# One head of each pair turned by DMA instead of TensorE in a latent-attention block

## The chip, the cores and the metric

The kernel runs on one core of a Trainium2 chip, in one launch. The metric is the device time of that core in microseconds (us). Five engines work side by side, each through its own instructions in order: TensorE (PE; its weight loads are listed apart as PEld), VectorE (DVE), ScalarE (ACT), GpSimd (POOL) and SyncE (SP), which here issues every DMA. They meet only at semaphores.

## The reference

The input is x of 1024 rows by 512. It is normalised by rows (xn), and the output is x + attention(xn) + experts(xn).

```
q_lat = rmsnorm(xn @ q_a_w, q_a_norm_w)            # 192 wide
q     = (q_lat @ q_b_w) -> 32 heads x (128 + 64)   # q_nope, q_pe; rope on q_pe
ckv   = xn @ kv_a_w                                # 64 latent + 64 for k_pe (rope)
kv    = rmsnorm(kv_lat, kv_a_norm_w) @ kv_b_w      # k_nope, v of 32 heads
scores = (q_nope.k_nope + q_pe.k_pe) * 192**-0.5
idx   = sum over 16 heads of iw * relu(iq . ik)    # the indexer
mask  = top 128 of idx in each causal row
attn  = softmax(where(mask, scores, -inf))
out   = (attn @ v) @ o_w
experts: top 2 of 8 gates, rank 16 each, added in
```

## The kernel before, in words

**Numbers.** A product that must keep 32-bit accuracy is made of three 16-bit ones: each operand is split into a high part (rounded to 16 bit) and a low part (what is left), and high x high, high x low and low x high are added up in PSUM. So every operand of TensorE needs a copy to 16 bit (`copy`, L712, on ACT) and a subtraction (`low`, L929, on DVE).

**Stages.** Projections and the indexer come first (to about 300 us), then the head loop (L658 on TensorE), then the last products with the output weights (L685).

**The head loop.** 32 heads make 16 pairs, and the 1024 query rows make two halves of four tiles of 128 rows. A *unit* is one pair in one half: 8 *steps*, one for each head and tile, in order. There are 32 units (NU): 16 of the low half, whose tiles see 128 to 512 keys, then 16 of the high half, whose tiles see 640 to 1024 keys. 256 steps (STEPS) in all. A step g goes through these hands:

- TensorE: scores of 128 rows by all keys seen (`scores`, L604, matmuls at L621), three steps ahead (AHEAD).
- DVE: `row_max` (L1123, instruction at L1131) adds the mask, scales, writes the tile in fp32 to one of four buffers `pr` and keeps the row's extreme `nmax`.
- ACT: `exp_step` (L879, L883): the exponential in place, with the row's sum, two steps ahead.
- TensorE: turns the probabilities block by block (128 x 128, fp32) into a PSUM bank of psT (L666), up to four blocks a bank.
- ACT: `p_hi_chunk` (L886) copies a bank, scaled by 1024, to the high part in `pT`. DVE: `p_low_chunk` (L1135) makes the low part.
- TensorE: `values` (L631, L640), three matmuls for each block of 128 keys, one step later.

In a step of the high half the turn needs two banks, so two copies on ACT and two subtractions on DVE. Between the steps of a unit stand five smaller jobs on the same three psT banks, in the order of the list RING (L255): "R" and "L" (`q_job`, the rope part and the latent part of the queries two units later, L539 to L543), "V" (`vo_pair`, L628, low half only), "O" (`out_T`, L649, the finished unit turned). `unit_out` (L1141) divides a unit's values by the row sums. In the low half DVE also finds the top 128 of the two largest mask rows between the steps (`top_part`, L1061 and L1068, in MARK_STEPS, 64 parts over steps 0 to 118).

POOL works on the queries two units ahead: rope (L1309 to L1313) and the low parts (L1318, L1322), and L1326 in the low half. SP issues the DMAs that this needs: `swap` (L339, L340: neighbouring rows exchanged), `place` (L349: rows to the other 64 partitions, 4 for each unit), and in the low half the loads at L371 and L372 and the store at L376.

The order is written out by hand in each engine's program; no scheduler changes it.

## Time and profile before

| what | value |
|---|---|
| three runs, us | 965.91, 969.08, 969.91 (median 969.08) |
| the profiled execution | 972.53 us, its span 970.8 us |
| PE busy | 880.3 us, 91% of the span |
| DVE busy | 740.9 us, 76% |
| ACT busy | 645.6 us, 67% |
| POOL busy | 367.4 us, 38% |
| mean granted TensorE clock | 0.972 of full |
| share of the 16 DMA engines in use by the SP queue | 25.4% |

The shares are means over stages that have different limits, so the head loop has to be read by its halves. In the profile's 40 slices TensorE is at 9 tenths in nearly every slice from the 21st on, while DVE is at 8 or 9 from the 7th to the 33rd. The last three slices are the output products, on TensorE alone.

### The profile page before, as it was taken

The page shows a single profiled execution, that of the slowest core. Times are in us where ns is not written, and L with a number is a line of the kernel's source. Part 1 is how long each engine was busy: PE and PEld are TensorE (multiplying, and loading weights), DVE is VectorE, ACT ScalarE, POOL GpSimd, SP SyncE. Part 2 cuts the span into 40 slices and gives each one's busy share as a digit, 9 for nine tenths or more (in the row PEclk, how much of TensorE's full clock was granted, in tenths as well). Part 3 has the DMA queues.
Part 4 walks back from the last instruction along what each step waited for, and adds up shares of the span by engine and source line. Part 5 has one row for each costly group of instructions (what it writes and reads, how often), then busy time and mean ns, then how long its engine had stood idle before and what let it go on. Part 6 is the DMA issues. An engine that isn't in the chain of part 4 may idle for free. (4 is left out here: it accounts for less than half of the span.)

```text
span 970.8 us, 21012 instructions
## 1 busy us (share of the span) xinstructions
PE 880.3 (91%) x7912; PEld 549.2 (57%) x7912; DVE 740.9 (76%) x1625; ACT 645.6 (67%) x1448; POOL 367.4 (38%) x291
## 2 busy tenths in 40 slices
PE   5979989968776989898889999999999999999998
PEld 2545544434443555555555777777777767774443
DVE  5366687899998999999998888888788888881100
ACT  3657799865674786777777777777777777880000
POOL 2093388754453544644554322322322323200000
PEclk9989999988886999999999999999999999999999
DMA  7012211112323145345443221111111111330111
GB/s 234 23 44 78 64 46 53 60 38 64 103 87 101 45 126 136 93 114 137 132 106 105 60 52 45 35 34 34 35 42 38 34 45 42 93 130 1 66 44 43
DMA packets 68259, 69.43 MB, mean 72 GB/s; under 512 B 8000, under 2 KB 50368, under 8 KB 68160
## 3 DMA queue, kind: packets, MB, share of 16 engines
q1 hardware_dynamic: 68160, 68.10, 25.4%
q8 instruction: 63, 1.03, 0.5%
q14 instruction: 36, 0.29, 0.1%
HBM read 36.62 MB, written 6.29 MB: 44 GB/s over the span
## 5 line engine op out<-in xcount | busy, mean ns | idle before, releaser
L712 ACT ACTIVATE arena<-psT 128x512 f16<-128x512 f32 (+4 forms) x516 | 242.8, 512 | 81.7 <-PE psT L666 71.4
L883 ACT ACTIVATE arena<-arena,small 128x512 f32<-128x512 f32 (+7 forms) x256 | 198.5, 775 | 65.0 <-DVE small L1131 64.4
L929 DVE SCALAR_TENSOR_TENSOR arena<-psT,arena 128x512 f16<-128x512 f32 (+3 forms) x392 | 206.2, 553 | 41.2 <-ACT arena L712 40.0
L621 PE MATMUL psS<-keyT,arena 128*128 128x512 f16 (+3 forms) x1152 | 231.7, 329 | 3.3 <-issue 3.3
L1131 DVE CUSTOM_DVE_ANT_0 arena<-psS,bias 128x512 f32<-128x512 f32 (+7 forms) x256 | 191.9, 750 | 37.4 <-PE psS L621 36.3
L666 PE MATMUL psT<-ident,arena 128*128 128x128 f32 x1152 | 177.4, 281 | 2.8 <-ACT arena L883 2.4
L621 PEld LDWEIGHTS psS<-keyT,arena 128*128 128x128 f16 x1152 | 102.9, 98 | 82.2 <-issue 25.8
L507 PE MATMUL psS<-ikT,big 128*128 128x512 f16 (+3 forms) x528 | 113.0, 362 | 30.7 <-DVE bias L1014 27.2
L640 PEld LDWEIGHTS psO<-val,arena 128*128 128x128 f16 x2976 | 109.6, 98 | 36.7 <-DVE arena L929 10.5
L666 PEld LDWEIGHTS psT<-ident,arena 128*128 128x128 f32 x1152 | 123.9, 141 | 4.9 <-ACT arena L883 2.3
L640 PE MATMUL psO<-val,arena 128*128 128x64 f16 x2976 | 118.3, 193 | 5.1 <-DVE arena L929 4.7
L1291 POOL TENSOR_TENSOR bias<-arena,bias 128x768 f32<-128x768 f32 (+2 forms) x48 | 91.3, 1917 | 47.1 <-ACT arena L778 46.5
L507 PEld LDWEIGHTS psS<-ikT,big 128*128 128x128 f16 x528 | 51.8, 105 | 85.0 <-DVE bias L1014 34.9
L1068 DVE MATCH_REPLACE8 bias<-m,bias 128x768 f32<-128x768 f32 (+4 forms) x112 | 89.9, 808 | 0.0
L1061 DVE MAX8 m<-bias 128x8 f32<-128x768 f32 (+4 forms) x112 | 87.4, 816 | 0.4
L1311 POOL TENSOR_TENSOR arena<-arena,sq 128x512 f32<-128x512 f32 x32 | 40.8, 1275 | 118.1 <-DMA arena<-arena 118.1
L929 DVE SCALAR_TENSOR_TENSOR big<-psT,big 128x512 f16<-128x512 f32 (+1 forms) x64 | 41.9, 655 | 40.6 <-ACT big L712 40.1
L1318 POOL TENSOR_TENSOR arena<-arena 128x512 f16<-128x512 f32 x32 | 37.1, 1158 | 88.8 <-DVE arena L1098 88.8
L712 ACT ACTIVATE big<-psT 128x512 f16<-128x512 f32 (+1 forms) x64 | 36.2, 565 | 51.3 <-PE psT L649 23.9
L1322 POOL TENSOR_TENSOR arena<-arena 128x512 f16<-128x512 f32 x32 | 37.8, 1181 | 79.9 <-ACT arena L712 78.8
L1309 POOL TENSOR_TENSOR arena<-arena,cq 128x512 f32<-128x512 f32 x32 | 40.9, 1278 | 71.0 <-ACT arena L712 71.0
L1225 POOL TENSOR_TENSOR arena<-arena 128x512 f16<-128x512 f32 x32 | 37.1, 1159 | 54.8 <-ACT arena L712 54.6
(150 smaller groups left out, 1147.9 us busy)
## 6 DMA issues: line engine op xcount, KB each, us to landing
arena<-arena SPq DMA_DIRECT2D x192, 128.0 KB, 2.4
arena<-in_wiq SPq DMA_DIRECT2D x32, 256.0 KB, 2.7
arena<-in_ow SPq DMA_DIRECT2D x16, 512.0 KB, 4.1
arena<-in_qbT SPq DMA_DIRECT2D x16, 256.0 KB, 2.5
wvo_parts<-arena SPq DMA_DIRECT2D x16, 256.0 KB, 2.7
arena<-in_qpe SPq DMA_DIRECT2D x16, 128.0 KB, 2.9
arena<-in_x SPq DMA_DIRECT2D x8, 256.0 KB, 2.9
out<-arena SPq DMA_DIRECT2D x8, 256.0 KB, 2.0
```

What stands on the lines that cost most here:

```text
L507: last = mm(bank[:, c:c + w], iq[:, a, n, t * P:(t + 1) * P], ikT[:, b, c:c + w], start=(a, b) == (0, 0), stop=(a, b) == (1, 0))
L621: last = mm(bank[:, k:k + w], Q[:, u % 2, a, h, q:q + P], keyT[:, b, h, k:k + w], start=(a, b) == (0, 0), stop=(a, b) == (1, 0))
L640: last = mm(dst, pT[:, g % 2, a, j * P:(j + 1) * P], val[:, b, j, :], start=j == 0 and n == 0, stop=j == nb - 1 and n == 2)
L666: last = nc.tensor.transpose(bank[:, (j % 4) * P:(j % 4 + 1) * P], pr[:, g % 4, j * P:(j + 1) * P], ident[:])
L712: return nc.scalar.activation(dst, src, ACT.Copy, scale=scale)
L883: nc.scalar.activation(pr[:, g % 4, 0:kw], pr[:, g % 4, 0:kw], ACT.Exp, bias=nmax[:, g % 4:g % 4 + 1], scale=-1.0, accum_out=rsum[:, unit_ ...
L929: return v.scalar_tensor_tensor(out=dst, in0=src, scalar=scale, in1=hi, op0=ALU.mult, op1=ALU.subtract)
L1061: v.max(m8[:, slot], bias[:, TOFF[t]:TOFF[t + 1]]).then_inc(tk_max, 1)
L1068: v.match_replace(out=row, in_to_replace=m8[:, slot], in_values=row, imm_value=TAKEN).then_inc(tk_rep, 1)
L1131: v.tensor_tensor_reduce(out=pr[:, g % 4, 0:kw], in0=bank[:, 0:kw], in1=bias[:, TOFF[t]:TOFF[t + 1]], scale=-c_s, scalar=3e38, op0=ALU.add ...
L1291: g.tensor_tensor(row, src[:, 0:P * (t + 1)], row, ALU.add).then_inc(sum_done, 1)
L1309: g.tensor_tensor(rt, raw, cq[:, cs], ALU.mult).then_inc(rot, 1)
```

## The change

In every unit the heads alternate: step s of a unit now belongs to head s % 2 and tile s // 2 (`head_of`, `tile_of`, `col_of`), where before the first four steps were one head. Even steps, the first head, go as before. Odd steps, the second head (`turns`, TURNED), are turned by DMA:

- DVE adds log(1024) to the row's extreme (`nmax_s`, one 128x1 instruction that waits for the one before it), so that the exponential comes out scaled.
- ACT, after the exponential and behind a wait for it, copies the rows as they stand to 16 bit (`rows_hi_`, one instruction of full width).
- POOL subtracts to get the low part (`rows_lo_`, one instruction of full width).
- SP issues one DMA transpose of both parts (`turn`), 2 x (blocks seen) blocks of 128 x 128 in 16 bit, into one of four buffers `cols`.
- TensorE forms the value products four steps later (LAG), so an odd step forms two sets and an even step none.

With this PSUM banks are shared out anew: in the high half the ring uses two banks and the third holds the values of every other unit. `pr`'s buffer is freed by POOL for a turned step. `unit_out` moves from step 0 to step 4 of the next unit and first multiplies the reciprocals by a constant (`scaled`). "O" and "V" change places. The buffers of `ow_s`, `wv_s`, `vo_s` and `vo32` become single to make room; the Q tiles are laid out head first. On POOL and SP the query work of a unit is spread over the steps. At the end the first output product goes ahead of the last two sets of values.

The diff, cut to its core:

```diff
+LOG_PR = math.log(PR_S)
+LAG = 4
+TURNED = ((1, 3, 5, 7), (1, 3, 5, 7))
...
+        rows_low = (ikf[:, 0:S], ikf[:, S:2 * S], view(6784, S, F16))
+        rows_high = (bias[:, 0:S].bitcast(F16), view(6784, 2 * S, F16), ikf)
+        cols_low = [view(at, S, F16) for at in (8832, 9344, 16000, 16512)]
+        cols_high = [view(at, 2 * S, F16) for at in (8832, 16000, 14976, 7808)]
...
         def tile_of(g):
-            return ORDERS[half_of(g)][g % 4]
+            return ORDERS[half_of(g)][g % 8 // 2]
+        def turns(g):
+            return g % 8 in TURNED[half_of(g)]
         def chunks(g):
-            return half_of(g) + 1
+            return 0 if turns(g) else half_of(g) + 1
+        def due(x):
+            return [g for g in (x - 1, x - LAG) if 0 <= g < STEPS and turns(g) == (g == x - LAG)]
...
+            def turn(g):
+                d, nb = TURN_AT[g], tile_of(g) + 1
+                sp.wait_ge(row_lo, d + 1)
...
+                elif d >= 4:
+                    sp.wait_ge(av_mm, summed(BY_DMA[d - 4]))
+                sp.dma_start_transpose(cols_of_turn(d)[:, 0:2 * nb * P].rearrange("p (j q) -> p j q", q=P),
+                                       rows_of_turn(d)[:, 0:2 * nb * P]).then_inc(landed[d % 4], 16)
...
+            for g in range(STEPS):
+                u, s = divmod(g, 8)
+                if turns(g):
+                    turn(g)
+                if s == 1 and 2 <= u + 1 < NU:
+                    place(u + 1, latent, qa_lo, q_lat, 1)
+                if s == 2 and 2 <= u + 1 < NU:
+                    place(u + 1, turned, q_rot, q_tur, 0)
+                if s == 3 and u + 2 < NU:
+                    swap(u + 2)
...
             def values(g):
-                pe.wait_ge(p_lo, TCUM[g + 1])
+                if turns(g):
+                    d = TURN_AT[g]
+                    pe.wait_ge(landed[d % 4], landed_by(d))
+                    src = cols_of_turn(d)[:, 0:2 * nb * P].rearrange("p (s k) -> p s k", s=2)
+                else:
+                    pe.wait_ge(p_lo, TCUM[g + 1])
+                    src = pT[:, FLIP_AT[g] % 2]
...
-                if g:
-                    values(g - 1)
-            values(STEPS - 1)
+                for late in due(g):
+                    values(late)
...
+            def rows_hi_(g):
+                kw, d = P * (tile_of(g) + 1), TURN_AT[g]
+                if d >= 3:
+                    act.wait_ge(landed[(d - 3) % 4], landed_by(d - 3))
...
+                act.wait_ge(exp_done, g + 1)
+                copy(rows_of_turn(d)[:, 0:kw], pr[:, g % 4, 0:kw], 1.0).then_inc(row_hi, 1)
...
-                if g >= 4:
+                if g >= 4 and turns(g - 4):
+                    dve.wait_ge(row_lo, TURN_AT[g - 4] + 1)
+                elif g >= 4:
                     dve.wait_ge(t_mm, TCUM[g - 3])
...
+                if turns(g):
+                    dve.wait_ge(max_done, g + 1)
+                    v.tensor_scalar(nmax_s[:, g % 4:g % 4 + 1], nmax[:, g % 4:g % 4 + 1], LOG_PR, None, ALU.add).then_inc(nmax_done, 1)
...
+            def rows_lo_(x):
+                kw, d = P * (tile_of(x) + 1), TURN_AT[x]
+                pool.wait_ge(row_hi, d + 1)
+                g.tensor_tensor(rows_of_turn(d)[:, kw:2 * kw], pr[:, x % 4, 0:kw], rows_of_turn(d)[:, 0:kw],
+                                ALU.subtract).then_inc(row_lo, 1)
```

TensorE in the high half before: the values of one step (L640), the turn of the next (L666), a query job (L539 to L543), scores (L621), again values and a turn.

```order
L640 MATMUL psO<-val,arena 128x64 x18
L666 MATMUL psT<-ident,arena 128x128 x5
L539 MATMUL psT<-qlT,w1hi 128x512
L540 MATMUL psT<-qlT,w1hi 128x512
L541 MATMUL psT<-qlT,w1lo 128x512
L542 MATMUL psT<-qlT,w2s 128x512
L543 MATMUL psT<-qlT,w2s 128x512
L621 MATMUL psS<-keyT,arena 128x512 x6
L640 MATMUL psO<-val,arena 128x64 x24
L666 MATMUL psT<-ident,arena 128x128 x7
```

TensorE at a like place of the changed kernel (L613 to L617 is the query job, L694 scores, L721 values, L748 the turn, L730 the finished unit turned).

```order
L613 MATMUL psT<-qlT,w1hi 128x512
L614 MATMUL psT<-qlT,w1hi 128x512
L615 MATMUL psT<-qlT,w1lo 128x512
L616 MATMUL psT<-qlT,w2s 128x512
L617 MATMUL psT<-qlT,w2s 128x512
L694 MATMUL psS<-keyT,arena 128x512 x6
L721 MATMUL psT<-val,arena 128x64 x45
L748 MATMUL psT<-ident,arena 128x128 x6
L694 MATMUL psS<-keyT,arena 128x512 x6
L730 MATMUL psT<-ident,arena 128x128 x4
```

Two sets of values (21 and 24 matmuls) stand together behind the scores of an odd step; there is a turn in every other step only.

ScalarE in the high half before: exponentials (L883), each between the copies of a turned step (L712, 512 columns and the rest).

```order
L883 ACTIVATE arena,small<-arena,small 128x1024
L712 ACTIVATE arena<-psT 128x512
L712 ACTIVATE arena<-psT 128x256
L883 ACTIVATE arena,small<-arena,small 128x640
L712 ACTIVATE big<-psT 128x512
L712 ACTIVATE arena<-psT 128x512 x2
L883 ACTIVATE arena,small<-arena,small 128x896
```

ScalarE at a like place of the changed kernel (L972 the exponential, L797 `copy`; a copy to arena, ikT or bias from arena is the new copy of rows).

```order
L972 ACTIVATE arena,small<-arena,small 128x896 x2
L797 ACTIVATE arena<-arena 128x896
L797 ACTIVATE arena<-psT 128x512
L797 ACTIVATE arena<-psT 128x384
L972 ACTIVATE arena,small<-arena,small 128x768 x2
L797 ACTIVATE ikT<-arena 128x768
```

Two exponentials of the same width now stand together, with one full-width copy behind the second and the two copies out of PSUM behind that.

## Rows read from the trace of the kernel before

**Rows 1.** Windows (us, busy and count by engine, clock, DMA share, GB/s).
```profile
339.00:450.00 111.00, 98.63 (x976) 59.69 (x974) 105.71 (x275) 82.89 (x240) 58.12 (x49) 1.00 0.44 117
620.00:710.00 90.00, 90.00 (x1113) 66.16 (x1112) 74.39 (x149) 70.10 (x147) 25.79 (x21) 1.00 0.15 37
```

**Rows 2.** Timeline of DVE, low half, line L1144 (start us, us, instruction).
```profile
338.62 0.19 DVE L1144 RECIPROCAL small<-small 128x8 f32<-128x8 f32 x1
...
449.90 0.18 DVE L1144 RECIPROCAL small<-small 128x8 f32<-128x8 f32 x1
```

**Rows 3.** Timeline of DVE, high half, line L1149.
```profile
556.67 0.69 DVE L1149 TENSOR_TENSOR arena<-psO,small 128x512 f32<-128x512 f32 x1
...
841.98 0.69 DVE L1149 TENSOR_TENSOR arena<-psO,small 128x512 f32<-128x512 f32 x1
```

**Rows 4.** Waits from 540 to 870 us (total us, times, longest).
```profile
ACT arena L712 <- PE psT L666: 63.7, 91, 1.2
...
DVE arena L1131 <- PE psS L621: 31.8, 43, 1.3
```

**Rows 5.** Waits from 339 to 450 us.
```profile
POOL arena L1311 <- DMA arena<-arena: 44.8, 8, 6.5
ACT arena L883 <- DVE small L1131: 26.6, 25, 2.2
```

**Rows 6.** Timeline of the high half, TensorE's matmuls.
```profile
762.60 1.07 PE L666 MATMUL psT<-ident,arena 128*128 128x128 f32 x8
...
763.50 1.14 PE L621 MATMUL psS<-keyT,arena 128*128 128x512 f16 x6
...
764.48 0.69 PE L640 MATMUL psO<-val,arena 128*128 128x64 f16 x18
...
765.00 0.74 PE L666 MATMUL psT<-ident,arena 128*128 128x128 f32 x5
...
765.59 0.38 PE L539 MATMUL psT<-qlT,w1hi 128*128 128x512 f16 x1
```

**Rows 7.** Groups by form from 460 to 870 us (busy us, mean ns; idle before).
```profile
L712 ACT ACTIVATE arena<-psT 128x512 f16<-128x512 f32 x192 | 110.9, 595 | 64.7 <-PE psT L666 64.6
L929 DVE SCALAR_TENSOR_TENSOR arena<-psT,arena 128x512 f16<-128x512 f32 x165 | 110.8, 687 | 23.0 <-ACT arena L712 22.0
...
L883 ACT ACTIVATE arena<-arena,small 128x1024 f32<-128x1024 f32 x32 | 36.8, 1151 | 0.2 <-DVE small L1131 0.2
...
L929 DVE SCALAR_TENSOR_TENSOR arena<-psT,arena 128x128 f16<-128x128 f32 x41 | 11.5, 281 | 0.0
L712 ACT ACTIVATE arena<-psT 128x128 f16<-128x128 f32 x41 | 11.1, 271 | 0.0
```

**Rows 8.** Groups by form of POOL over the whole run.
```profile
L1291 POOL TENSOR_TENSOR bias<-arena,bias 128x1024 f32<-128x1024 f32 x16 | 37.7, 2355 | 29.0 <-ACT arena L778 28.4
L1318 POOL TENSOR_TENSOR arena<-arena 128x512 f16<-128x512 f32 x32 | 37.1, 1158 | 88.8 <-DVE arena L1098 88.8
...
L1236 POOL TENSOR_TENSOR arena<-arena,small 128x128 f32<-128x128 f32 x8 | 2.9, 403 | 0.0
```

**Rows 9.** DMA from 12 to 14.5 us (packets, MB, share of 16 engines).
```profile
DMA packets 2543, 0.51 MB, mean 203 GB/s; under 512 B 2362, under 2 KB 2475, under 8 KB 2543
...
q1 hardware_dynamic: 2543, 0.51, 106.6%
```

**Rows 10.** DMA from 339 to 450 us: queue, packets, MB, share.
```profile
q1 hardware_dynamic: 10080, 12.85, 43.8%
```

**Rows 11.** DMA from 600 to 710 us.
```profile
q1 hardware_dynamic: 3680, 3.93, 15.0%
```

**Rows 12.** DMA over the whole run: the queue; issues by KB and us to landing.
```profile
q1 hardware_dynamic: 68160, 68.10, 25.4%
...
arena<-arena SPq DMA_DIRECT2D x192, 128.0 KB, 2.4
```

**Rows 13.** Timeline of SP's issues, high half.
```profile
604.25 0.60 SPq L340 DMA_DIRECT2D arena<-arena  x1
```

More of the change, by code:

```diff
@@ L381, in _ @@
             load_ow(0)
-            load_ow(1)
-            for u in range(NU - 2):
-                swap(u + 2)
-                place(u + 2, latent, qa_lo, q_lat, 1)
-                place(u + 2, turned, q_rot, q_tur, 0)
-                if 1 <= u <= NP:
-                    store_vo(u - 1)
-                if 1 <= u < NP - 1:
+            for g in range(STEPS):
[8 more added lines that the diff above has]
+                    swap(u + 2)
+                if s == 4 and u + 1 < NP:
                     load_ow(u + 1)
-            for u in range(2):
-                sp.wait_ge(vo_st[u], 16 * NP // 2)
+                if s == 7 and u < NP:
+                    store_vo(u)
             sp.wait_ge(qa_mm, NU)
@@ L658, in _ @@
             for g in range(STEPS):
-                pe.wait_ge(exp_done, g + 1)
+                if not turns(g):
+                    pe.wait_ge(exp_done, g + 1)
                 for use in uses_of(g):
@@ L694, in _ @@
             pe.wait_ge(max_done, STEPS)
-            for t in range(2):
-                products(t, t, range(NP))
-                experts(t, t)
+            products(0, 0, range(NP))
+            experts(0, 0)
+            for g in range(STEPS, STEPS + LAG):
+                for late in due(g):
+                    values(late)
+            products(1, 1, range(NP))
+            experts(1, 1)
             pe.wait_ge(p_lo, TCUM[STEPS])
@@ L896, in ot_evac @@
                 copy(big[:, 0, p, c * CH:(c + 1) * CH], bank[:], O_S / (PR_S * K_S)).then_inc(ot_hi, 1)
-            exp_step(0)
-            exp_step(1)
+            for g in range(AHEAD - 1):
+                exp_step(g)
+                if turns(g):
+                    rows_hi_(g)
             for g in range(STEPS):
+                for use in uses_of(g):
+                    what, at, c = use
+                    if what == "T":
+                        p_hi_chunk(psT[BANK[use]], g, c)
+                if g + AHEAD - 1 < STEPS:
+                    exp_step(g + AHEAD - 1)
+                    if turns(g + AHEAD - 1):
+                        rows_hi_(g + AHEAD - 1)
                 for use in uses_of(g):
@@ L904, in _ @@
                     if what == "T":
[L905 to L907 removed]
+                        continue
                     elif what == "O":
@@ L1334, in _ @@
                     rope_low((8, 13).index(n))
-            for u in range(2, NU):
-                rope_turn(u)
-                q_low(u)
-                rope_low(u)
-                if u - 2 < NP:
-                    vo_low(u - 2)
+            for x in range(STEPS):
+                u, s = divmod(x, 8)
+                if x + 1 < STEPS and turns(x + 1):
+                    rows_lo_(x + 1)
+                if s == 0 and 2 <= u + 1 < NU:
+                    rope_low(u + 1)
+                if s == 3 and u + 2 < NU:
+                    rope_cos(u + 2)
+                if s == 5 and u + 2 < NU:
+                    rope_sin(u + 2)
+                if s == 6 and u < NP:
+                    vo_low(u)
+                if s == 7 and u + 2 < NU:
+                    q_low(u + 2)
 def kernel(**inputs):
```

209 lines of the change are left out of this document (135 added, 74 removed).

## The prediction

> **What bounds the kernel now.** I read the windows first, one in each half of the head loop, because the page's shares mix stages. The first of the two rows [rows 1] is the low half: DVE is busy 105.7 of 111 us (95%), TensorE 89%, ACT 75%, POOL 52%. The second is the high half: TensorE is busy all 90 of 90 us, DVE 83%, ACT 78%, POOL 29%. So two different engines set the two halves, at a granted clock of 1.00 of full in both (the 2.4 GHz level).
>
> Next the length of a unit of 8 steps. In the low half the reciprocal that closes a unit comes at 338.62 and, eight units on, at 449.90 [rows 2]: 13.91 us a unit. In the high half the division comes at 556.67 and, 13 units on, at 841.98 [rows 3]: 21.95 us a unit.
>
> Last the waits. In the high half ACT's copies wait 63.7 us for TensorE's turns and DVE's row extremes 31.8 us for its scores [rows 4]: the others wait for TensorE. In the low half ACT's exponentials wait for DVE, and POOL waits 44.8 us for the swap DMA, 5.6 us of each unit's 13.9 [rows 5].
>
> **What leaves TensorE.** Eight turns of blocks run from 762.60 to the start of the scores at 763.50, 0.90 us, and five from 765.00 to 765.59, 0.59 us [rows 6]. That is 0.103 us a block and 0.07 us a step (eight of them show as 1.07 us busy, since each overlaps what follows). In a high unit the four turned steps have 5 + 6 + 7 + 8 = 26 blocks: 26 x 0.103 + 4 x 0.07 = 2.98 us less. The value products are the same matmuls, only later. A high unit falls to 18.97 us if TensorE stays the bound. In a low unit 1 + 2 + 3 + 4 = 10 blocks go, 1.3 us by the same slope.
>
> **DVE.** A turned step loses its subtractions, 0.687 us for 512 columns and 0.281 us for 128 [rows 7]. For 640 to 1024 columns that is about 0.97, 1.10, 1.24 and 1.37, together 4.7 us a high unit; for 128 to 512 columns 0.28 + 0.42 + 0.55 + 0.68 = 1.9 us a low unit. What is added is small: four 128x1 instructions and one 128x8 product. The trace has none of 128x1 with such a wait; the nearest is the reciprocal of 128x8 at 0.19 us [rows 2]. Bounds 0.08 (free but for a start) and 0.35 (with a stall for the one before it); I take 0.2 each, 1.0 us a unit. Low unit: 105.7/8 = 13.2 busy, less 1.9, plus 1.0, is 12.3; with the 5% of idle that it has now, 13.0. High unit: 74.4/90 x 21.95 = 18.1, less 4.7, plus 1.0, is 14.4, off the path.
>
> **ACT.** It has 70.1/90 x 21.95 = 17.1 us of work in a high unit [rows 1]. For a turned step the two copies out of PSUM (0.595 and 0.27 to 0.595) become one out of SBUF of 640 to 1024 columns. The nearest row for one wide instruction out of SBUF is the exponential, 1.151 us for 1024 [rows 7], against 2 x 0.595 = 1.19 for the two. I take no difference, bounds -0.2 and +0.2 us each. The wait for the exponential just ahead is new; behind it are queued the copies of the next turn, for which DVE and TensorE wait. Price 0.1 to 0.4, taken 0.2 x 4 = 0.8 us. 17.9 us is under 18.97, but only just: what hides it is TensorE, and of the gain 1.1 us a unit is all the cover left.
>
> **POOL.** New are four subtractions a unit. By width 2.355 us for 1024, 1.158 for 512 and 0.403 for 128 [rows 8], so about 7.8 us a high unit and 3.3 a low one. With 25.8/90 x 21.95 = 6.3 and 58.1/8 = 7.3 there now [rows 1], 14.1 of 19 and 10.6 of 13. DVE's next row extreme waits for this subtraction where it waited for TensorE, and behind POOL's wait for the swap DMA the next subtraction is queued. That wait is 5.6 us now; spread over the steps it should be hidden by the two steps between the swap and its use, and costs what is left of it if not.
>
> **DMA.** This is the unknown: the trace has no transpose. A turned step moves two parts (high and low) of each of its blocks, 32 KB each: in a high unit 2 x 26 = 52 such blocks, 1.7 MB, in a low one 20, 0.65 MB. If a row of a block (128 elements of 2 bytes, 256 B) is a packet, each of the 16 engines has 8 packets a block. The nearest row is the stretch of small packets at 12 to 14.5 us: 2543 packets, 2362 of them under 512 B, in 2.5 us at a full queue [rows 9], so 16 x 1.066 x 2.5 / 2543 = 16.8 ns of an engine for each, 0.134 us a block. The other end is the mean over all packets of the run, 0.254 x 16 x 970.8 / 68160 = 57.9 ns [rows 12], 0.46 us a block. The lower end takes four rows in one packet of 1 KB at 16.8 ns, 0.034 us a block. I take 0.134, as the row of like packets. The queue then has 52 x 0.134 = 7.0 us plus 15% of 21.95 = 3.3 [rows 11] of 19 us in a high unit, and 20 x 0.134 = 2.7 plus 43.8% of 13.91 = 6.1 [rows 10] of 13 in a low one. It is hidden. A plain DMA of 128 KB lands 2.4 us after issue [rows 12]; the rows are ready about when TensorE starts the step, and values come four steps later, 9.5 us in the high half and 6.5 in the low. SP's own issue is 0.60 us [rows 13]; 10 in a high unit are 6.0 us, 13 in a low one 7.8. The copy, subtraction and turn together have to be slower than three steps before TensorE or ACT (which waits for the landing three turns back) feels it.
>
> Of this the Trainium skill speaks against the change: "VectorE: DVE Perf Modes", section The three transpose paths, gives 1309 ns for a 128x128 block by DMA and 390 ns by TensorE. By that figure taken block after block the turns of a high unit would be an estimated 52 x 1.309 = 68 us. For TensorE the trace disagrees (0.10 us a block in a row of them), so that figure looks like the time of one block alone; for the DMA no run here shows it. If it held, the turns' rival below would be at its far end.
>
> **The rest.** Single buffers for the output weights: load, product, two copies, subtraction and store follow each other once a unit, with about 13 us for some 10; no cost taken, up to 1 us a low unit if the store is late. Two ring banks in the high half: between two turns there is now a whole step without one, over 2 us, against a copy and subtraction of about 1.8; no cost, up to 0.5 a unit. The end, with two sets of values behind a product: within 1 us.
>
> **The sum.** High: 2.98 less 0.5 for coupling that I can't price (ACT at 94% of TensorE) is 2.45 a unit, x 16 = 39 us. Low: 13.91 to 13.0, 0.9 x 15 units with mask work = 13.5 us. Together 52. The profiled execution took 972.5 us, 3.4 above the median of the runs; on the median, 969.1 - 52 = 917 us.
>
> **Rivals.**
>
> *The other engines take the pace, not the DMAs.* In the high half ACT's wait for its own exponential, and for a landing, costs 0.7 a turned step in place of 0.2: 17.1 + 2.8 = 19.9 us, with some 4% idle 20.7, a gain of 1.25 x 16 = 20 us. In the low half DVE's wait for POOL eats the rest. 969 - 20 = 949 us. For it: ACT's narrow margin, and all engines in order with four buffers. Against it: the exponential is two steps ahead.
>
> *The turns themselves set the pace, and the kernel is slower.* Place: the SP queue, its issue or its 16 engines. The change breaks even where a high unit's queue is as long as the unit is now: (21.95 - 3.3) / 52 = 0.36 us a block. Below 0.31 the gain is whole, so the step between is steep. At 0.40, between that and the slow end of 0.46, a high unit is 20.8 + 3.3 = 24.1, 2.2 x 16 = 34 us more, a low one 8.0 + 6.1 = 14.1, some 4 us in all: 1007 us. At 0.46 it is 24.1 + 3.3 = 27.4 and 9.3 + 6.1 = 15.4: 87 and 24 us more, 1080 us. And if the blocks of a turn went one after another, each at the time in which a whole DMA of 32 to 128 KB could land, over 1 us, it would be above 1500 us. For it: a DMA that writes one element of a row to each partition has no like in the trace, its issue may grow with the number of blocks (a plain one's does not), and the trace shows that packets here do cost 58 ns on the mean. Against it: those packets are 1 KB on the mean, and small ones went at 16.8.
>
> The Trainium skill's page "DMA: Bandwidth & Descriptors", section "Why a DMA increments its semaphore by 16 and not by 1", has a table by which earlier chips issue an SBUF to SBUF transpose in small tiles one after another, 262,144 sequencer cycles for 8,192 of them. The size of a tile isn't given, so no time follows from it; it would be this rival by way of SP, and no row shows it.
>
> **Chances.** The forecast has 0.50, with its own range 903 to 935. The engines' rival has 0.14, of which 0.02 ends within 0.5% of before. The turns' rival has 0.36, of which 0.03 ends within 0.5% and 0.02 is the case of block after block. So faster by over 0.5% is 0.62, within 0.5% (what a measurement can tell from no change here) 0.05, slower 0.33. The range starts at 903, under which 0.05 is left, and runs into the turns' rival to 1020, above which are 0.12.
>
> **What would show it.** Right: high units of 19 to 20 us with TensorE still at 95% or more, low units near 13, the transposes landing within 6 us of issue, no wait of ACT or TensorE for a DMA. TensorE or ACT waiting for a transpose, SP busy most of the unit, or landings over 9 us show the slower rival. TensorE at 90% in the high half with short DMAs shows the other. Wrong is also a low unit that stays at 13.9: then DVE's saving went into waits for POOL.

## The result, and the profile after

The changed kernel takes 1062.07 us (median of 4 runs, 1060.82 to 1064.28) against 969.50 for the kernel before, run beside it (4 runs, 965.91 to 973.71): 1.0956 of it, with a 95% interval of 1.0908 to 1.1003. The forecast was 917 us, the range 903 to 1020. It is slower by 93 us and outside the range.

Where the time went shows in the exponentials, since both kernels do them in the order of the steps and two steps ahead. The division that closes a unit (`unit_out`) can't bound the stretches, because the change moved it by half a unit. The first exponential of unit 0 and of unit 16 (the first of the high half) and the last one, before:

```profile
306.94 0.72 ACT L883 ACTIVATE arena<-arena,small 128x512 f32<-128x512 f32 x1 [5.25 <-DVE small L1131]
...
529.41 1.15 ACT L883 ACTIVATE arena<-arena,small 128x1024 f32<-128x1024 f32 x1 [0.20 <-DVE small L1131]
...
872.32 0.94 ACT L883 ACTIVATE arena<-arena,small 128x768 f32<-128x768 f32 x1
```

The same of the changed kernel.

```profile
305.40 0.72 ACT L972 ACTIVATE arena<-arena,small 128x512 f32<-128x512 f32 x1 [5.53 <-DVE small L1242]
...
557.21 1.15 ACT L972 ACTIVATE arena<-arena,small 128x1024 f32<-128x1024 f32 x1 [2.47 <-DVE small L1242]
...
940.68 0.94 ACT L972 ACTIVATE arena<-arena,small 128x768 f32<-128x768 f32 x1 [0.99 <-DVE small L1247]
```

| stretch | before | after | difference |
|---|---|---|---|
| start to the first exponential of unit 0 | 306.9 | 305.4 | -1.5 |
| from there to the first of unit 16 (low half) | 222.5 | 251.8 | +29.3 |
| from there to the last exponential (high half) | 342.9 | 383.5 | +40.6 |
| from there to the end of the span | 98.5 | 118.3 | +19.8 |
| span | 970.8 | 1059.0 | +88.2 |

All further times of a stretch are measured in this way. For the time of one unit the divisions serve, as in [rows 3]: units 0, 11, 16 and 29 of the changed kernel.

```profile
330.84 0.69 DVE L1265 TENSOR_TENSOR arena<-psS,small 128x512 f32<-128x512 f32 x1
...
507.49 0.69 DVE L1265 TENSOR_TENSOR arena<-psO,small 128x512 f32<-128x512 f32 x1
...
604.33 0.69 DVE L1265 TENSOR_TENSOR arena<-psT,small 128x512 f32<-128x512 f32 x1
...
920.22 0.69 DVE L1265 TENSOR_TENSOR arena<-psO,small 128x512 f32<-128x512 f32 x1
```

A unit takes 176.65 / 11 = 16.06 us in the low half (13.91 in [rows 2]) and 315.89 / 13 = 24.3 in the high one (21.95 in [rows 3]). All further unit times are measured between these divisions. The windows of the two halves (columns as in [rows 1]) show that no engine is full.

```profile
331.00:507.00 176.00, 132.82 (x1222) 74.91 (x1219) 140.79 (x387) 121.07 (x329) 114.22 (x110) 0.91 0.63 145
604.00:920.00 316.00, 262.00 (x3208) 171.63 (x3207) 206.74 (x430) 224.49 (x416) 167.79 (x116) 0.98 0.55 103
```

In the high half TensorE is busy 262 of 316 us (83%; 100% in [rows 1]), ACT 71%, DVE 65%, POOL 53%; in the low half DVE 80% (95% before) and TensorE 75%, at a granted clock of 0.91. The queue and the landings of the transposes (median us in the last column), from the DMA view of 604 to 920 us:

```profile
q1 hardware_dynamic: 94272, 32.12, 53.9%
...
arena<-bias SPq DMA_TRANSPOSE x18, 3.9
arena<-arena SPq DMA_TRANSPOSE x18, 4.0
arena<-ikT SPq DMA_TRANSPOSE x17, 4.2
```

So the turns land in about 4 us, values use them four steps later, and the queue is half idle. The waits from 604 to 920 us (total us, times, longest) name no transpose, but DVE and ACT waiting for each other:

```profile
ACT arena L972 <- DVE small L1247: 59.6, 53, 1.4
DVE arena L1038 <- ACT arena L797: 52.7, 39, 1.8
...
PE psT L748 <- DVE big L1038: 33.5, 13, 2.6
```

L972 is the exponential, L1247 the new shift of the row's extreme, L797 `copy`, L1038 `low`. One pair of steps with 1024 columns, from the timeline of all engines (some rows left out):

```profile
731.23 1.22 DVE L1242 CUSTOM_DVE_ANT_0 arena<-psS,bias 128x1024 f32<-128x1024 f32 x1
...
732.50 0.15 DVE L1247 TENSOR_SCALAR small<-small 128x1 f32<-128x1 f32 x1
...
732.68 1.15 ACT L972 ACTIVATE arena<-arena,small 128x1024 f32<-128x1024 f32 x1 [1.25 <-DVE small L1247]
...
734.02 1.06 ACT L797 ACTIVATE arena<-arena 128x1024 f16<-128x1024 f32 x1
734.98 0.58 ACT L797 ACTIVATE big<-psT 128x512 f16<-128x512 f32 x1
735.15 2.13 POOL L1459 TENSOR_TENSOR arena<-arena 128x1024 f16<-128x1024 f32 x1 [3.92 <-ACT arena L797]
...
735.59 0.69 DVE L1038 SCALAR_TENSOR_TENSOR big<-psT,big 128x512 f16<-128x512 f32 x1 [2.14 <-ACT big L797]
736.20 1.36 DVE L1207 CAST arena<-arena 128x512 f16<-128x512 f32 x1
...
736.34 0.66 PE L748 MATMUL psT<-ident,arena 128*128 128x128 f32 x4 [2.57 <-DVE big L1038]
...
737.03 0.60 ACT L797 ACTIVATE arena<-psT 128x512 f16<-128x512 f32 x1 [0.98 <-PE psT L748]
...
738.68 0.81 DVE L1242 CUSTOM_DVE_ANT_0 arena<-psS,bias 128x640 f32<-128x640 f32 x1
```

This is a closed ring: row extreme, shift, exponential, rows copy (734.02, the new one), the finished unit's copy (734.98) and its low part, which free a ring bank, a turn on TensorE (736.34), its copy (737.03), its low part, and only then the row extreme of the next turned step (738.68). It takes 7.45 us for these two steps (the mean of a unit's four pairs is 24.3 / 4 = 6.1), with all engines idle for parts of it. ACT first sits idle for 1.25 us, waiting for the shift, and then does the rows copy while all others wait for what is queued behind it.

### The profile page after: what moved, and what is told of

It is laid out like the page before. It is cut to its first block, busy times and chain, and to the rows that moved or that the text cites. A ratio compares the mean times of both kernels' runs of the same rounds, so it can differ in the third digit from the quotient of the medians.

```text
span 1059.0 us, 20025 instructions
## 1 busy us (share of the span) xinstructions
PE 844.3 (80%) x7336; PEld 489.9 (46%) x7336; DVE 696.3 (66%) x1593; ACT 659.1 (62%) x1384; POOL 528.9 (50%) x429
## 4 chain that ended last, share of the span: by engine, by line
PE 37%; DVE 28%; ACT 14%; issue 13%; POOL 5%; DMA 1%; SPq 0%; POOLq 0%; ACTq 0%; DVEq 0%
PE psS L766 8%; DVE arena L1242 7%; PE psS L694 7%; ACT arena L972 6%; ACT arena L797 5%; DVE arena L1038 4%; DVE m L1170 4%; DVE bias L1177 3%; PE psT L548 3%; PE psT L748 3%; ACT big L797 2%; PE psS L581 2%; DVE arena L1207 2%; PE psO L721 2%; PE psT L568 2%
## 5 line engine op out<-in xcount | busy, mean ns | idle before, releaser
L972 ACT ACTIVATE arena<-arena,small 128x512 f32<-128x512 f32 (+7 forms) x256 | 198.5, 776 | 144.2 <-DVE small L1247 131.2
L694 PE MATMUL psS<-keyT,arena 128*128 128x512 f16 (+3 forms) x1152 | 236.6, 337 | 12.7 <-issue 9.8
L797 ACT ACTIVATE arena<-psT 128x512 f16<-128x512 f32 (+4 forms) x324 | 156.0, 526 | 45.6 <-PE psT L748 35.5
L1038 DVE SCALAR_TENSOR_TENSOR arena<-psT,arena 128x512 f16<-128x512 f32 x200 | 106.4, 557 | 94.9 <-ACT arena L797 94.4
L694 PEld LDWEIGHTS psS<-keyT,arena 128*128 128x128 f16 x1152 | 106.1, 101 | 103.8 <-issue 37.6
L748 PE MATMUL psT<-ident,arena 128*128 128x128 f32 x576 | 98.2, 292 | 44.1 <-DVE big L1038 42.6
L1459 POOL TENSOR_TENSOR ikT<-arena,ikT 128x512 f16<-128x512 f32 (+5 forms) x64 | 72.3, 1130 | 99.6 <-ACT ikT L797 98.8
L1038 DVE SCALAR_TENSOR_TENSOR big<-psT,big 128x512 f16<-128x512 f32 (+1 forms) x64 | 42.1, 657 | 81.6 <-ACT big L797 81.4
L1459 POOL TENSOR_TENSOR arena<-arena 128x384 f16<-128x384 f32 (+7 forms) x42 | 53.5, 1273 | 74.4 <-ACT arena L797 74.1
L721 PE MATMUL psO<-val,arena 128*128 128x64 f16 x1728 | 68.8, 196 | 25.1 <-DVE arena L1038 25.1
L748 PEld LDWEIGHTS psT<-ident,arena 128*128 128x128 f32 x576 | 63.9, 146 | 51.5 <-DVE big L1038 42.0
L721 PEld LDWEIGHTS psO<-val,arena 128*128 128x128 f16 x1728 | 62.1, 100 | 37.9 <-DVE arena L1038 30.7
L797 ACT ACTIVATE big<-psT 128x512 f16<-128x512 f32 (+1 forms) x64 | 35.9, 561 | 69.5 <-PE psT L730 41.7
L797 ACT ACTIVATE arena<-arena 128x512 f16<-128x512 f32 (+3 forms) x106 | 65.0, 645 | 5.1 <-DMA arena<-in_wiq 1.0
L1459 POOL TENSOR_TENSOR bias<-arena,bias 128x1024 f16<-128x1024 f32 (+3 forms) x22 | 39.1, 1776 | 57.7 <-ACT bias L797 57.7
```

What stands on the lines that cost most here:

```text
L694: last = mm(bank[:, k:k + w], Q[:, u % 2, h, a, q:q + P], keyT[:, b, h, k:k + w], start=(a, b) == (0, 0), stop=(a, b) == (1, 0))
L721: last = mm(dst, src[:, a, j * P:(j + 1) * P], val[:, b, j, :], start=j == 0 and n == 0, stop=j == nb - 1 and n == 2)
L748: last = nc.tensor.transpose(bank[:, (j % 4) * P:(j % 4 + 1) * P], pr[:, g % 4, j * P:(j + 1) * P], ident[:])
L797: return nc.scalar.activation(dst, src, ACT.Copy, scale=scale)
L972: nc.scalar.activation(pr[:, g % 4, 0:kw], pr[:, g % 4, 0:kw], ACT.Exp, bias=shift[:, g % 4:g % 4 + 1], scale=-1.0, accum_out=rsum[:, unit ...
L1038: return v.scalar_tensor_tensor(out=dst, in0=src, scalar=scale, in1=hi, op0=ALU.mult, op1=ALU.subtract)
```

## The experiments

Theories: **ring**, the order on ACT and DVE as above; **turns**, the prediction's rival, the DMA or SP's issue; **small edits**, the shift and the product with constants. In the expectations the ring is theory L, its part in the ring banks B, the turns T; O is the new order of heads and buffers, Q queries placed late, P the product, E the late loads. Medians, each against the kernel before in the same batch:

| kernel | us | of before | 95% | low unit | high unit |
|---|---|---|---|---|---|
| e1 max first | 1110.17 | 1.1414 | 1.1373-1.1455 | 15.5 | 27.9 |
| e2 copy later | 1002.88 | 1.0314 | 1.0275-1.0353 | 15.3 | 21.1 |
| e3 both | 1109.12 | 1.1428 | 1.1356-1.1500 | 15.5 | 27.9 |
| e4 second turn | 1104.17 | 1.1342 | 1.1282-1.1402 | 18.6 | 24.2 |
| e5 no turns | 1075.82 | 1.1081 | 1.1036-1.1127 | 14.95 | 27.7 |
| e6 e2, no shift | 998.31 | 1.0292 | 1.0237-1.0347 | 15.5 | 20.9 |
| e7 e2, jobs first | 980.33 | 1.0096 | 1.0058-1.0134 | 15.25 | 19.9 |
| e8 e2, high only | 998.88 | 1.0289 | 1.0235-1.0343 | 14.95 | 21.2 |
| e9 e7, queries first | 962.66 | 0.9900 | 0.9849-0.9950 | 14.5 | 19.7 |
| e10 e5, no product | 1057.74 | 1.0867 | 1.0805-1.0928 | 13.95 | 27.2 |
| e11 e9, tensor_scalar | 962.70 | 0.9908 | 0.9872-0.9945 | 14.4 | 19.7 |
| e12 e11, high only | 959.50 | 0.9858 | 0.9809-0.9907 | 13.65 | 19.7 |
| e13 after, loads early | 1044.90 | 1.0762 | 1.0719-1.0805 | 16.1 | 24.3 |
| e14 e11, loads early | 954.85 | 0.9806 | 0.9769-0.9843 | 14.5 | 19.7 |
| e15 e12, loads early | 945.64 | 0.9737 | 0.9714-0.9761 | 13.6 | 19.8 |

### e1, e2, e3: which order closes the ring

e1, on DVE: the row extreme goes ahead of the low parts of the step's turn.

```
+                if g + AHEAD < STEPS:
+                    row_max(g + AHEAD)
                 for use in uses_of(g):
                     if what == "T":
                         p_low_chunk(psT[BANK[use]], g, c)
-                if g + AHEAD < STEPS:
-                    row_max(g + AHEAD)
```

> On DVE the row extreme of step g+3 now goes ahead of the subtraction(s) of step g; nothing else differs from the changed kernel (1062 us; 24.0 us a high unit, about 15.9 a low one). Theory L (a loop between DVE and ACT sets the pace: subtraction of g, row extreme of g+3, its shift, exponential of g+3, copy of its rows, a small job's copy, copy of the turned g+2, subtraction of g+2): the subtraction leaves the piece ahead of the exponential, up to 1.2 us of each pair of steps in the high half and 0.5 in the low, so high units near 21 to 22 us, low near 14.5 to 15, in all 1000 to 1025 us. Theory B (two ring banks in the high half make TensorE wait): the banks come free later, so high units stay at 24 or grow, low ones stay; 1060 or more. Theory T (the DMA turns set the pace): no change, 1062.

e2, on ACT: the rows copy of a turned step is done one step later, ahead of that step's exponential.

```
+                if g and g + AHEAD - 2 < STEPS and turns(g + AHEAD - 2):
+                    rows_hi_(g + AHEAD - 2)
                 if g + AHEAD - 1 < STEPS:
                     exp_step(g + AHEAD - 1)
-                    if turns(g + AHEAD - 1):
-                        rows_hi_(g + AHEAD - 1)
```

> On ACT the copy of a turned step's rows moves from right behind its own exponential to behind the copy out of PSUM of the next step. Theory L: the copy (0.75 to 1.06 us and the 0.25 of its wait) leaves the piece between the exponential and the next copy out of PSUM, in both halves: high units 21 to 22 us, low near 15, in all 1005 to 1030 us. Theory B: the small jobs' copies come earlier and free their banks about 1 us sooner, so the high half gains and the low half, with three banks, does not: 1030 to 1045. Theory T: the turns start a step later, so the same or up to 10 us slower.

e3 has both edits.

> Both order changes at once. Theory L: the two gains add up until TensorE or ACT is the bound, high units 20 to 21 us, low 13.5 to 14.5: 965 to 995 us. Theory B: no better than the copy moved alone. Theory T: no change.

Measured: e1 is 48 us slower than the changed kernel, e2 59 us faster, e3 no better than e1. So the rows copy's place on ACT is the largest single cause, and the loop as I had first drawn it was wrong in its DVE part: putting 1.2 us of row extreme ahead of the low parts makes a high unit 27.9 us. The low parts are what frees a ring bank and lets values start. The profile of e1 fits this reading: its low half, with three ring banks, is 10.0 us shorter than the changed kernel's, its high half, with two, 57.8 longer, and there TensorE's query job waits for low parts 43.6 us from 604 to 920 us, where it waited 19.4 in the changed kernel. The same pair of steps in e2, from its timeline of DVE and ACT:

```profile
718.28 1.23 DVE L1242 CUSTOM_DVE_ANT_0 arena<-psS,bias 128x1024 f32<-128x1024 f32 x1
...
719.74 1.15 ACT L972 ACTIVATE arena<-arena,small 128x1024 f32<-128x1024 f32 x1 [0.35 <-DVE small L1247]
...
720.88 0.58 ACT L797 ACTIVATE big<-psT 128x512 f16<-128x512 f32 x1
...
722.10 0.42 DVE L1207 CAST arena<-arena 128x512 f16<-128x512 f32 x1
...
723.43 1.05 ACT L797 ACTIVATE ikT<-arena 128x1024 f16<-128x1024 f32 x1
...
724.17 0.81 DVE L1242 CUSTOM_DVE_ANT_0 arena<-psS,bias 128x640 f32<-128x640 f32 x1
```

From extreme to extreme it is 5.89 us where it was 7.45. The rows copy (723.43) now runs while DVE makes low parts and the next extreme, and the wait for the shift fell from 1.25 to 0.35. The edit also moves POOL's subtraction. The cast at 736.20 ran beside that subtraction and took 1.36 us, as all 13 did in the changed kernel from 604 to 920 us; in e2 it takes 0.42 in all 13 from 590 to 850 us. Up to 0.94 of the 3.2 us that a high unit fell may be this, and no run separates it from the place on ACT.

### e4: the DMA's share, doubled

Behind each turn SP issues a second one of the same size, from a tensor at rest into a spare one.

```
+                sp.dma_start_transpose(spare[:, 0:2 * nb * P]..., keyT[:, 0]...[:, 0:2 * nb * P]).then_inc(extra, 16)
```

> A second DMA transpose of the same size, from constant keys to a spare buffer, behind every turn, so SP issues twice as much and the DMA engines turn twice as much. Theory T: each of the 128 extra turns costs its own time on SP or the queue, 1.2 us of issue at least, so 1062 + 150 us or more. Theories L and B: the queue has room (54% in use in the high half, of which turns are some 40), so within 10 us of 1062 in the high half, and a few us more in the low one, where it is 61% in use: 1062 to 1085.

Its windows (high half, then low):

```profile
644.00:959.00 315.00, 260.02 (x3168) 170.12 (x3167) 206.12 (x429) 223.59 (x414) 168.42 (x116) 0.98 0.97 173
332.00:516.00 184.00, 127.64 (x1120) 74.50 (x1120) 131.18 (x354) 110.46 (x300) 103.89 (x100) 0.87 0.74 160
```

The DMA engines are now 97% busy in the high half (55% before the edit), and a high unit stays at 24.2 us. There the turns' theory is out. In the low half a unit grows by 2.5 us. A likely reason, not tested alone, is that the swaps and places of the queries share the queue and SP with the turns. So that half has no room for twice the turns; what single ones cost there e12 shows.

### e5, e8, e10: with fewer turns

e5 keeps the orders, the two ring banks, the alternating heads and the product with constants, but TensorE turns every step.

```
-TURNED = ((1, 3, 5, 7), (1, 3, 5, 7))
+TURNED = ((), ())
```

> The changed kernel in all but the turning: no step is turned by DMA, all 256 by TensorE as before, with the heads alternating, two ring banks in the high half, the unit closed at step 4 and the query work spread. Theory L: with a turn and its copy in every step the loop between DVE and ACT has the slack that it had before, so the low half, whose banks are three as before, is back at 13.9 to 14.3 us a unit. Its high half has two banks for twice the turns, so TensorE waits for a bank in every step: 24 to 27 us a unit. Rival O (the new order and single buffers cost the low half its time, and not the DMA-turned steps): the low half stays at 15 to 16 us.

A high unit takes 27.7 us, 5.7 more than before the change. So with all turns on TensorE the new layout, two ring banks and alternating heads together, is far worse than the old one (e5 doesn't separate the two), and half the turns by DMA earn some 3.4 us of that back even in the bad order. The low half gave the second finding. The closing of a unit there, from its timeline:

```profile
450.45 1.27 POOL L1439 TENSOR_TENSOR arena<-arena 128x512 f32<-128x512 f32 x1
...
450.63 1.11 DVE L1260 TENSOR_TENSOR small<-small 128x8 f32<-128x8 f32 x1
```

L1260 is the product of 128x8 numbers with constants. It ends at 451.74, as POOL's instruction does at 451.72. In e5's groups by form from 361 to 497 us it takes 0.98 us on average, where a reciprocal of the same size took 0.19 us [rows 2]:

```profile
L1260 DVE TENSOR_TENSOR small<-small 128x8 f32<-128x8 f32 x10 | 9.8, 976 | 0.3
```

e10 is e5 without the product (its factor is 1 there).

> The run with no turns (1076 us; low units 15.1) without the product of the reciprocals with the constants, which takes 0.98 us there for 8 columns since it ends when POOL's instruction of the time ends. All steps are turned by TensorE, so the constants are all 1 and nothing that is computed changes. Theory P: low units fall by the product and its wait, 1.1 us, to 14.0: 16 x 1.1 = 18 us; the high half, bound by its banks, stays at 27.6: about 1058. Theory Q: the low half stays at 15.1, since without turns no DMA stands ahead of the queries: 1070 to 1076.

It is 18 us faster than e5, and a low unit falls from 14.95 to 13.95. So where DVE sets the pace, that one small instruction costs 1.0 us a unit.

e8 is e2 with DMA turns in the high half alone.

```
+TURNED = ((), (1, 3, 5, 7))
```

> On top of the copy moved later (1003 us): only the high half is turned by DMA, the low half wholly by TensorE. Theory L: low units back at about 14 us from 15.4, 16 x 1.4 = 22 us less, high ones at 21.3 as in the run with the copy moved: 978 to 984. Rival O: the low half stays at 15.4: 1000 to 1005.

998.88 against 1002.88, from separate batches and with ratios that overlap: no clear gain, the low unit at e5's 14.95.

### e6, e7, e9: what is left of the ring

e6 is e2 without the shift (the scale of the turned rows is left out of the exponential, so those rows come out unscaled).

```
-                v.tensor_scalar(nmax_s[...], nmax[...], LOG_PR, None, ALU.add).then_inc(nmax_done, 1)
```

> On top of the copy moved later (1003 us): the shift by log(1024) is left out, so the exponential waits for the row extreme alone, and the 128 small instructions on DVE with their wait go; the turned probabilities carry no factor of 1024 in 16 bit, which is all that differs in what is computed. Theory L: 0.25 us out of the loop between extreme and exponential in each pair: 4 x 0.25 x 32 = 32 us at most where the loop binds, 10 to 25 us taken: 978 to 993. Theory B, for the high half: nothing there, since the bank is freed by ACT and DVE work behind it, 995 to 1003.

1.0292 against e2's 1.0314: no difference that can be told. The waits that carried the shift's name were waits for the row extreme ahead of it.

e7 is e2 with the small jobs' copies ahead of the exponential on ACT, and the finished unit's low part ahead of the row extreme on DVE.

```
                     rows_hi_(g + AHEAD - 2)
+                for use in uses_of(g):   # O, V, R, L
+                    ...
                 if g + AHEAD - 1 < STEPS:
                     exp_step(g + AHEAD - 1)
```

> On top of the copy moved later (1003 us): in an odd step ACT copies the small job's bank ahead of the exponential, and DVE subtracts for the finished unit ahead of the row extreme. Theory B (after the copy is moved, the high half, at 21.3 us a unit against 19.0 of TensorE work, waits for a ring bank): the bank of the finished unit comes about 1.2 us sooner, high units 20 to 20.6 us, and 985 to 992 in all. Theory L: the exponential comes later by the wait for TensorE's job, so high units stay at 21.3 or grow, 1003 to 1020.

22 us less than e2, the high unit at 19.9. What is left is in the low half. Its waits from 330 to 500 us, and its timeline:

```profile
PE psS L694 <- issue: 23.2, 10, 3.4
```
```profile
462.27 1.24 SPq L447 DMA_TRANSPOSE arena<-ikT  x1
...
463.60 2.46 SPq L403 DMA_DIRECT2D arena<-arena  x4
...
467.98 0.81 PE L694 MATMUL psS<-keyT,arena 128*128 128x512 f16 x3 [3.34 <-issue]
```

The scores of a unit's first step wait 3.3 us. The view gives no releaser, but the `place` DMAs (L403) that bring a unit's queries are issued only from 463.60 to 466.06, behind a turn, and a DMA of their size lands 2.4 us after its issue [rows 12]. e9 tests this: all of them are issued in step 0 ahead of the turn, and POOL makes the queries' low parts ahead of the rows' low part.

```
-                if turns(g):
-                    turn(g)
-                if s == 1 and 2 <= u + 1 < NU:
+                if s == 0 and 2 <= u + 1 < NU:
                     place(u + 1, latent, qa_lo, q_lat, 1)
-                if s == 2 and 2 <= u + 1 < NU:
                     place(u + 1, turned, q_rot, q_tur, 0)
+                if turns(g):
+                    turn(g)
```

> On top of the copy later and the jobs first (980 us): SP issues the four DMAs that place the next unit's queries ahead of that unit's first turn, not behind it, and POOL makes their low part ahead of the rows' low part. In the low half of the run before, TensorE stood 23.2 us in ten waits ahead of a unit's first scores, up to 3.4 us, that the profile gives to nothing on an engine, just until a placing DMA lands. Theory Q (queries placed too late): these go, low units 15.4 to about 14.0, 1.4 x 16 = 22 us: 955 to 965. Theory P (what is left in the low half is DVE's product standing behind POOL and the loop): the waits go elsewhere, 975 to 980.

18 us less than e7, 12.4 of it in the low half by the profiles, and the wait of 23.2 us is no longer among the longest there. The share of POOL's new order in this wasn't measured apart. At 0.9900 (0.9849 to 0.9950) the kernel is now faster than before the change. The high unit is at 19.7 us. A window of 220 us in e9's high half:

```profile
600.00:820.00 220.00, 215.85 (x2737) 144.90 (x2736) 169.80 (x367) 184.82 (x356) 146.21 (x100) 1.00 0.69 128
```

TensorE is busy 98% of it: the bound that the forecast had counted on.

### e11, e12: the product, and the low half

e11 is e9 with the product on four columns and an immediate number.

```
-                v.tensor_tensor(rinv, rinv, scaled[:, u // NP], ALU.mult).then_inc(ri_done, 1)
+                v.tensor_scalar(rinv[:, 4:8], rinv[:, 4:8], PR_S, None, ALU.mult).then_inc(ri_done, 1)
```

> Copy later, jobs first, queries first, and the product with the constants as a one-operand multiplication of the four columns that need it. Both halves turned by DMA. Q and P together: low units 13 to 13.5, high 19.5 to 19.9: 935 to 950. If only Q holds, 955 to 965; if DVE's work and the loop still bind, 960 to 975.

No difference: in e9 POOL's work has moved and the product takes 0.167 us on average from 340 to 480 us, so there was nothing left to gain. With e10 this miss says that the price of the product hangs on what POOL does at that moment, and not on the instruction.

e12 is e11 with DMA turns in the high half alone, and no product in the low half.

> As the last, but the low half wholly turned by TensorE and without a product there. If what the new order cost the low half is the product alone, low units are 14.0 as in the run with neither, high ones 19.6: 16 x 2.3 = 37 us less than before in the high half and some 3 more in the low: 935 to 945. If the low half keeps another cost of the new order (15 us a unit), 955 to 965.

3 us less than e11, with overlapping ratios; its profiled head loop began 3.3 us later than e11's, which hides part of it. By the unit it is 13.65 us against 14.4, but over the whole low half only 221.0 against 226.1. So there, where TensorE is not the bound, DMA turns cost 0.3 us a unit on the mean and up to 0.75 in the best order (0.17 of it the product), and 13.65 is 0.26 less than before the change.

### e13, e14, e15: the end

Behind the last value the changed kernel loads the output weights. TensorE's timeline at 960 us:

```profile
960.05 4.77 PE L766 MATMUL psS<-w1hi,big 128*128 128x512 f16 x12 [14.37 <-DMA sq<-wvo_parts]
964.66 2.75 PE L766 MATMUL psS<-w1lo,big 128*128 128x512 f16 x12
```

SP's timeline shows why: the load stands behind the last turn.

```profile
944.39 1.43 SPq L447 DMA_TRANSPOSE arena<-bias  x1
945.87 0.89 SPq L471 DMA_DIRECT2D w1hi<-wvo_parts  x1
...
948.85 1.07 SPq L475 DMA_DIRECT2D sq<-wvo_parts  x1
```

e13 is the changed kernel with this block issued at the last unit's first step.

```
+                if g == 8 * (NU - 1):
+                    sp.wait_ge(qa_mm, NU)
+                    ...                     # the five loads of wvo_parts
```

> The changed kernel (1062 us), with SP's five loads of the output weights issued at the first step of the last unit, not behind the last turn; nothing else differs. Theory E (the loads queued behind the turns cost the end of the kernel): TensorE's wait of 14.4 us ahead of the first output product goes, and with it the low clock behind it, in which twelve matmuls took 4.8 us in place of 2.75: 1062 - 16 = 1046 us. Rival: the four steps that are still to come slow by the 4 MB beside them and give half back: 1054.

1044.90 against 1062.07: 17 us. In the profiles the end, from the last exponential on, falls from 118.3 to 104.1. The kernel before issued the same loads from 843.05 us on, 33.6 us ahead of their first use at 876.67. e14 and e15 are e11 and e12 with the same edit.

> All order changes with both halves turned (962.7 us), and the loads early: theory E 14 to 18 us less, 945 to 949. The rival: 955.

> The high half turned by DMA, the low half by TensorE (959.5 us), and the loads early: its wait is 16.2 us now, so theory E gives 941 to 945, against 971.6 before; high units stay at 19.8 and low ones at 13.8. The rival: 951.

954.85 and 945.64 us: 8 and 14 us less. The edit acts in the last unit alone, and in the profiles the end falls by 11.1 and 7.2 us. The rest of e15's 14 is a start 4.7 us earlier and a low half 2.3 shorter than e12's, which the edit doesn't touch. e15 beats both kernels: 0.9737 of before (0.9714 to 0.9761), and 116 us under the changed kernel by the medians. Its exponentials, as in the first table:

```profile
307.64 0.72 ACT L970 ACTIVATE arena<-arena,small 128x512 f32<-128x512 f32 x1 [5.46 <-DVE small L1237]
...
526.38 1.15 ACT L970 ACTIVATE arena<-arena,small 128x1024 f32<-128x1024 f32 x1 [2.05 <-DVE small L1237]
...
835.18 0.94 ACT L970 ACTIVATE arena<-arena,small 128x768 f32<-128x768 f32 x1
```

Its high half takes 308.8 us, 34.1 less than before; the low half 3.7 less; but the end 109.7, 11.2 more. The prediction's 39 us for the high half were 2.45 a unit; e15 gains 2.2 in a steady unit. At its end TensorE waits 7.25 us for the first turn of the last unit, which now stands behind the loads: its issue alone takes SP 10.95 us.

```profile
829.18 10.95 SPq L445 DMA_TRANSPOSE arena<-bias  x1
```
```profile
842.18 1.46 PE L719 MATMUL psO<-val,arena 128*128 128x64 f16 x24 [7.25 <-DMA arena<-bias]
```

## Why the prediction was wrong, step by step

- **What leaves TensorE: right.** 2.98 us a unit and a floor of 18.97 were forecast, 19.5 with coupling. With the orders mended a high unit is 19.7 us at 98% TensorE.
- **The DMA: right in kind.** The window of 604 to 920 us has 89,408 packets under 512 B. Taking [rows 11]' 15.0% of 21.95 us as 13.6% of 24.3, the turns have 40.3% of 316 us on 16 engines: 22.8 ns a packet, 0.18 us a block, between the 0.134 taken and the 0.36 of break-even. By the figure of the Trainium skill that the prediction quoted ("VectorE: DVE Perf Modes", The three transpose paths, 1309 ns a block), taken block after block, the turns would have set the pace; for turns of 10 to 16 blocks the trace disagrees, with 0.18.
- **SP's issue: a cost not seen.** A transpose takes SP 1.24 us in e7's row at 462.27 and 1.43 in the row at 944.39, where a plain DMA takes 0.60 [rows 13]. It set no pace by itself, but the places issued behind it were late (e9, 18 us, with POOL's new order in it).
- **DVE: additions half right.** A high unit has 206.74 / 316 x 24.3 = 15.9 us of DVE work, 14.4 were forecast. The shift takes 0.153 us (0.2 taken). The product takes 0.17 alone and up to 1.12 beside POOL, over the bound of 0.35. The 0.94 by which the cast grew beside POOL was left out.
- **ACT: where the forecast failed.** One wide copy takes 1.06 us for 1.19, as bounded. The wait of this copy for its own exponential was priced at 0.1 to 0.4 us a turned step, and is 0.1 (734.02 against the sum's end at 733.93). Not priced was the wait ahead of the exponential, for the new step's extreme and shift: 59.6 / 52 = 1.15 us a turned step. The prediction named what is queued behind the rows copy, but took its delay as hidden since ACT's sum (17.9 us; 17.3 measured) was under TensorE's. A sum of busy times says nothing of a ring: the rows copy lay in the chain between an extreme and the next one, which goes through both engines and the ring banks.
- **"Two ring banks in the high half": failed in this order.** "No cost, up to 0.5 a unit" was the text, from a copy and a subtraction of 1.8 us against a step of over 2. That leaves out that the bank's copy on ACT stands behind an exponential and a rows copy (2.4 us), so that TensorE waits 2.57 us for it once a unit (33.5 / 13). With the orders mended two banks do suffice: e9 has them, and TensorE is busy 98%. The mended orders (e2 59, e7 22, e9 18 us) give 99 us, by the profiles some 75 in the high half and 24 in the low.
- **"The end: within 1 us": failed.** From the last exponential on it is 19.8 us longer, and e13 takes 14.2 of that off. The loads need only the last unit's queries, but stand in SP's program behind the head loop, and that loop now ends with the last turn; the prediction looked at the values there and not at SP.
- **The low half: failed.** 13.0 us was forecast from DVE's busy time alone. The best with DMA turns is 14.4 (e11), without 13.65 (e12). What the prediction named as the sign of this, DVE waiting for POOL, is there: 11.7 us from 330 to 500 us in e9, beside waits of ACT and TensorE for DVE. How the saving splits between them wasn't measured.
- **The rivals.** The turns' one is out by e4. The engines' one had the right mechanism, but with a wait of 0.7 us and only on the gaining side (949 us). All of the slower side had been given to the DMA; that an order could cost more than TensorE gains had no chance.

The failed step is the term "less 0.5 for coupling that I can't price". It was 0.5 us a high unit, and with the changed kernel's orders it is 24.3 - 18.97 = 5.3, of which e2, e7 and e9 take 4.6 back by order alone. With it failed the end, taken as within 1 us and 19.8 longer, and the low half, taken as 0.9 us a unit shorter and 2.15 longer. That e15 lands under the old kernel shows the saving on TensorE was real; it doesn't make the forecast of this kernel right.

Left open: how much of e2's gain is the place on ACT and how much the cast that no longer meets POOL; what POOL's new order gives in e9; and how the low half's 0.3 to 0.75 us a unit divides between POOL, SP and the lower load of TensorE.

## What to carry to other kernels

When a change puts a new instruction between two that stand on different engines' in-order queues, follow the ring from one row extreme to the next by hand and add up its durations; if that sum is over the unit's time by the busiest engine, the ring is the bound however idle the engines look. Then put the new work where its engine was waiting (here the rows copy into ACT's 1.25 us of idle time), and put jobs that free a shared bank first. Take offload only in the stage whose bound engine it relieves, and look at what is queued behind it on the DMA-issuing engine, at the end of the kernel too.

## What the runs showed of the hardware

- **DVE is held up by POOL.** Beside the rows of e5 above, two from the changed kernel's timeline:

```profile
443.82 1.27 POOL L1439 TENSOR_TENSOR arena<-arena,sq 128x512 f32<-128x512 f32 x1 [2.08 <-DMA arena<-arena]
443.99 1.12 DVE L1260 TENSOR_TENSOR small<-small 128x8 f32<-128x8 f32 x1
```

  The DVE instruction starts inside POOL's and ends with it (445.11, 445.09); alone it takes 0.17. The cast of 128x512 (L1207), 0.42 us in e2's row at 722.10, takes 1.36 at 736.20 beside POOL's subtraction. Over all 32 its median is 1.10 in the changed kernel and 0.42 in the one before. The Trainium skill has this ("SBUF — State Buffer", section SBUF: two separate sides): the port pair that DVE and GpSimd share is an exclusive lock, held for a whole instruction by whichever starts first, a GpSimd instruction or a DVE one that has two SBUF inputs or runs in a two-port mode. The rows of the product, which has two SBUF inputs and starts second, agree. The change adds four subtractions of 1.40 to 2.13 us to POOL in a high unit.
- **DMA transposes in batches** of 2 to 16 blocks (two parts of each block of a step) land in 3.6 us at the median over the whole run (2.3 to 6.1) and in about 4 in the high half, at 0.18 us of all 16 engines a block in the high half.
- **The clock after a wait.** After the 14.37 us wait twelve matmuls take 4.77 us and the next twelve 2.75; the granted clock is 0.65 from 960 to 966 us. So this late load cost its wait and 2.0 us behind it. In e15, whose wait of 7.25 us ends 6.5 us before them, the same first twelve take 3.73 us.
